# Half of a batch's experts run inside its own second attention instead of the next batch's first; gates are made per half; narrow mix blocks become wide

## The chip, the cores and the metric

One core of one Trainium2 chip runs the whole program. The time is microseconds on the device from the start to the end of one execution. Engines: PE is TensorE (matmuls, with their weight loads apart as PEld), DVE is VectorE, ACT is ScalarE, POOL is GpSimd, SP is SyncE, which here only issues DMAs. Each engine runs its own instructions in order and waits on semaphores.

## What is computed

A batch of 8 images of 256 channels and 32 x 32 positions (T = 1024 tokens) goes through three layers, each added to its input:

```python
x = x + proj(attention(qkv(group_norm(x))))        # 8 heads of 32, no mask, all 1024 keys
t = t + W_O(attention(layer_norm(t)))              # 8 heads of 32, causal
sel = sigmoid(layer_norm(t) @ expert_sel.T)        # 32 experts
w = top-2 of sel per token, else 0                 # gates, [token, expert]
h = relu(einsum('td,edh->teh', layer_norm(t), keys))   # hidden size 64
t = t + einsum('teh,te,ehv->tv', h, w, values)     # all experts computed, gated
```

## The kernel before, in words

The layout is channels on partitions: 256 channels are two tiles of 128 (CT), which are also the two groups of four heads (g = 0, 1). Tokens are cut in two halves of 512 (hf = 0, 1), and 8 tiles of 128. A weight product is split in high and low parts and needs three matmuls (`split`, L532 to L537).

The order of the work is written out by hand as a list of steps in the class `Steps` (L47 to L141); each engine walks the same list and does its share of each step, so the order of the list is the order on every engine and on SP's queue. There are four lists: `first`, `head` (batch 0, no experts), `body` (batches 1 to 7, a loop of seven trips, which starts with the experts of the batch before) and `last` (the experts of batch 7 alone). A count of steps gives each semaphore value.

The steps that matter here:
- `qk` (L617, L817, L1034): the query or key projection of one group and half: six matmuls on PE, the high part on ACT, the low part on DVE, both into `nat`. `stack` (L432): SP copies `nat` into `q_st` and `k_st` with 12 DMAs of 128 KB. A later q step writes over `nat` and so waits on ACT for the other group's copies (L820 to L826).
- `top` (L638, L1042): scores of one query tile for two heads in one of two two-bank PSUM buffers (`ps_two`), and DVE's row maximum over them. `peak` joins the two key halves, `row` (L658, L836) turns the maxima into a row of `q_st` with PE and ACT. In attention 1 (the causal one) half 0 has 8 tops a group and half 1 has 16, eight of them over fewer keys.
- `mix` (L673, L844): scores the other way round, exp on ACT, then values and sums on PE into `ps_acc`. A wide block takes two heads in a `ps_two` buffer and two exps of up to 1024 columns; a narrow block one head in a `ps_one` buffer and four exps of up to 512. The four mixes of attention 1 are e (g 0, hf 0, wide), f (g 1, hf 0, narrow), g (g 0, hf 1, narrow) and h (g 1, hf 1, wide). `norm`, `div` and `fin` divide by the sums, mostly on DVE.
- `out`, `lna`, `lnb`: output projection with the residual, then the layer norm of one half: mean, squares, mean of squares, inverse root.
- `logits`, `inputs`, `turn` (L726, L903, L456): selection scores of all 1024 tokens (16 matmuls, of which the trace shows 32 passes), top two on DVE; high part (ACT) and low part (POOL) of the layer norm's output; the gates turned by PE, written to DRAM with eight DMAs, waited for, and read back broadcast over partitions, two DMAs for each expert tile, four tiles ahead.
- `up` (L742, L917, L1137): one of 16 expert tiles (two experts each) for one half: six matmuls up, DVE's relu times gate (L1146), ACT's high part, DVE's low part (L965), and with a lag of two tiles six matmuls down into `ps_acc`. POOL makes low parts of keys and values (L510). `down` finishes the last two and adds to `x_res`; SP stores.

Memory is shared: `gated` and the broadcast gates lie in `probs`, where the exps go (L312, L318), and the experts' parts lie in `nat` (L314 to L317).

In `body` the 32 ups (both halves of batch it-1) are spread among 70 of the 80 top steps of attention 0 (L97 to L108). The narrow mixes f and g leave `ps_two` free, so that the tops of (1,0,1) stand among f's last block and a projection (L128), and those of (1,1,1) among g (L129 to L131). h has the output projection of half 0, its layer norm and the next batch's group norm among its blocks (L133, L134).

```python
ups = [("up", hf, j) for hf in range(self.halves) for j in range(self.experts)]
steps = spread(ups, tops) if tops else ups
...
e, f, g, h = (self.mix(1, g, hf, hf == g) for hf in (0, 1) for g in (0, 1))
```

## Time and profile before

| | |
|---|---|
| median of 3 runs | 3903.73 us (3895.03 to 3910.25) |
| the profiled execution | 3897.4 us |
| its span | 3895.7 us, mean granted PE clock 0.892 |
| busy share of the span | PE 87%, DVE 52%, ACT 43%, POOL 11% |
| one trip of the loop | about 475 us |

The page gives each engine's busy time as a share of the span and then in 40 equal slices; the clock line is what TensorE was granted in each slice, in tenths of 2.4 GHz, and a stretch is at 2.4 or at 1.2 GHz, so a tenth in between is a mixture. A row of a window says how long each engine was busy in that stretch. In a timeline, the bracket behind a row is the time for which the engine stood idle before it, and what it waited for. "Idle" alone does not cost anything on an engine that is not the bottleneck.

### The profile page before, as it was taken

Reading aid. Unit: us, or ns where it says so; the run is one execution under the profiler, and the core shown is the slowest. Engines: PE = TensorE matmul, PEld = TensorE weight load, DVE = VectorE, ACT = ScalarE, POOL = GpSimd, SP = SyncE. Lnnn points to the kernel's source line nnn. Section 1 sums busy time; section 2 is a strip of 40 time slices with the busy share of each in tenths; the row PEclk is TensorE's granted clock in tenths of the full one; section 3 lists DMA queues with packets and bytes.
Section 4 is the critical chain, followed back from the end, with each engine's and each line's share of the span. In section 5 each row is a group of like instructions: output and inputs, shape, how many; then the busy total and the mean of one; then the engine's idle time right before and its main releaser. Section 6 shows DMA issues by size and latency. Waiting matters only on the chain.

```text
span 3895.7 us, 54844 instructions
## 1 busy us (share of the span) xinstructions
PE 3380.4 (87%) x18386; PEld 1841.5 (47%) x18386; DVE 2022.0 (52%) x2825; ACT 1670.6 (43%) x2604; POOL 421.5 (11%) x539
## 2 busy tenths in 40 slices
PE   5898799987998879988799888998889988899779
PEld 2343464445634356343563445534465344554347
DVE  6434583356823568235672447624575254843544
ACT  1453335543364433644236343463434634345334
POOL 0000030001300013000230002200032000310005
PEclk7797899988999789988899898997889978999789
DMA  3011340114402043020530205202142022511125
GB/s 98 1 44 33 87 140 25 44 33 114 132 6 60 18 127 120 9 57 17 141 111 17 58 19 145 90 17 60 29 142 82 17 60 46 148 58 33 45 52 167
DMA packets 151948, 263.13 MB, mean 68 GB/s; under 512 B 26832, under 2 KB 28880, under 8 KB 151504
## 3 DMA queue, kind: packets, MB, share of 16 engines
q1 hardware_dynamic: 151632, 259.15, 24.6%
q8 instruction: 170, 2.79, 0.3%
q14 instruction: 146, 1.20, 0.1%
HBM read 145.80 MB, written 9.44 MB: 40 GB/s over the span
## 4 chain that ended last, share of the span: by engine, by line
PE 69%; DVE 13%; ACT 7%; issue 6%; SPq 3%; DMA 2%; DVEq 0%; POOL 0%; ACTq 0%; POOLq 0%
PE ps_acc L583 10%; PE ps_two L688 8%; PE ps_acc L592 8%; PE ps_one L535 7%; DVE tops L1050 7%; PE ps_two L652 6%; PE ps_one L537 5%; PE ps_one L536 5%; PE ps_one L688 3%; PE ps_acc L535 3%; PE ps_acc L536 3%; PE ps_acc L537 3%; SPq L448 2%; ACT stacks L840 2%; ACT probs L857 2%
## 5 line engine op out<-in xcount | busy, mean ns | idle before, releaser
L1050 DVE TENSOR_REDUCE tops<-ps_two 128x2 bf16<-128x1024 f32 (+3 forms) x896 | 964.4, 1112 | 431.8 <-PE ps_two L652 253.8
L857 ACT ACTIVATE probs<-ps_two 128x1024 f32<-128x1024 f32 (+1 forms) x704 | 642.3, 961 | 287.9 <-PE ps_two L688 220.4
L652 PE MATMUL ps_two<-stacks 32*128 32x512 f32 (+3 forms) x1792 | 426.9, 508 | 175.7 <-DVE tops L1050 135.4
L688 PE MATMUL ps_two<-stacks 97*128 97x512 f32 (+3 forms) x1408 | 462.7, 439 | 63.8 <-ACT probs L857 34.3
L583 PE MATMUL ps_acc<-probs,v_sb 128*32 128x512 f32 (+3 forms) x3584 | 474.8, 605 | 0.0
L510 POOL TENSOR_TENSOR nat<-expert_sb,nat 128x256 fp32r<-128x256 f32 x512 | 382.1, 747 | 644.1 <-ACT nat L801 546.7
L592 PE MATMUL ps_acc<-probs,ones 128*32 128x512 f32 (+3 forms) x3584 | 451.3, 578 | 0.0
L688 PEld LDWEIGHTS ps_two<-stacks 97*128 97x128 f32 x1408 | 250.1, 196 | 333.4 <-issue 187.9
L652 PEld LDWEIGHTS ps_two<-stacks 32*128 32x128 f32 x1792 | 172.4, 204 | 456.3 <-DVE tops L1050 230.6
L801 ACT CAST nat<-expert_sb 128x256 fp32r<-128x256 f32 x256 | 103.1, 406 | 616.3 <-DVE probs L1146 531.8
L516 POOL TENSOR_TENSOR act_lo<-xn,act_hi 128x2048 fp32r<-128x2048 f32 x8 | 36.1, 4509 | 2822.7 <-ACT act_hi L907 2822.7
L1064 DVE COPY rsum<-ps_acc 128x512 f32<-128x512 f32 x64 | 44.2, 691 | 543.3 <-PE ps_acc L592 543.3
L857 ACT ACTIVATE probs<-ps_one 128x512 f32<-128x512 f32 (+3 forms) x384 | 169.8, 488 | 196.0 <-PE ps_one L692 97.2
L535 PE MATMUL ps_one<-act_hi,nat 128*128 128x512 f32 x512 | 232.1, 453 | 23.4 <-POOL nat L510 23.4
L840 ACT CAST stacks<-ps_two 1x1024 fp32r<-1x1024 f32 x128 | 128.6, 1005 | 266.4 <-PE ps_two L669 263.5
L1146 DVE SCALAR_TENSOR_TENSOR probs<-ps_one,probs 128x512 f32<-128x512 f32 x256 | 175.8, 687 | 126.2 <-PE ps_one L537 77.8
L592 PEld LDWEIGHTS ps_acc<-probs,ones 128*32 128x32 f32 x3584 | 114.3, 117 | 222.7 <-issue 215.6
L535 PE MATMUL ps_one<-act_hi,w_hi 128*128 128x512 f32 x392 | 178.5, 455 | 45.8 <-DVE act_lo L1032 16.9
L535 PE MATMUL ps_acc<-nat 128*128 128x512 f32 x512 | 209.2, 409 | 1.1 <-POOL nat L510 0.9
L537 PE MATMUL ps_one<-act_hi,nat 128*128 128x512 f32 x512 | 208.9, 408 | 0.0
L536 PE MATMUL ps_one<-act_lo,nat 128*128 128x512 f32 x512 | 208.4, 407 | 0.0
L536 PE MATMUL ps_acc<-nat 128*128 128x512 f32 x512 | 205.6, 402 | 0.0
(127 smaller groups left out, 4476.2 us busy)
## 6 DMA issues: line engine op xcount, KB each, us to landing
stacks<-nat SPq DMA_DIRECT2D x792, 128.0 KB, 2.4
expert_sb<-experts_dram SPq DMA_DIRECT2D x256, 256.0 KB, 2.8
probs<-gates_dram SPq DMA_DIRECT2D x512, 128.0 KB, 3.0
x_in<-x_in_dram SPq DMA_DIRECT2D x9, 1024.0 KB, 5.0
out_dram<-x_res SPq DMA_DIRECT2D x16, 512.0 KB, 2.9
probs<-mats_dram SPq DMA_DIRECT2D x1, 2048.0 KB, 9.3
gates_dram<-w_turn SPq DMA_DIRECT2D x64, 16.0 KB, 1.6
sel_w<-sel_dram SPq DMA_DIRECT2D x1, 32.0 KB, 8.3
```

The lines of the kernel that those rows point to most:

```text
L510: pool.tensor_tensor(parts[:, 2 + m % 2, :], expert_sb[:, m % RING, c:c + C], f(parts[:, m % 2, :]), ALU.subtract).then_inc(lowered, 1)
L535: pe.matmul(acc, lh, rh, start=start, stop=False)
L536: pe.matmul(acc, lh, rl, start=False, stop=False)
L537: return pe.matmul(acc, ll, rh, start=False, stop=stop)
L583: pe.matmul(ps_acc[HD * j:HD * j + HD, 0, a:HALF], v_sb[:, k, c:c + HD], probs[:, sec.no["mix"][s] % 2, j, a:HALF], start=(k == 0), stop=( ...
L592: mm = pe.matmul(ps_acc[HD * j:HD * j + HD, 1, a:HALF], ones32[:], probs[:, sec.no["mix"][s] % 2, j, a:HALF], start=(k == 0), stop=(k == l ...
L652: mm = pe.matmul(acc[:, HALF * e:HALF * e + n_keys], q_st[rows, g, j, P * i:P * i + P], k_st[rows, g, j, HALF * kh:HALF * kh + n_keys], st ...
L688: mm = pe.matmul(at[:, a:HALF], k_st[0:MID + 1, g, j, P * k:P * k + P], q_st[0:MID + 1, g, j, HALF * hf + a:HALF * hf + HALF], start=True, ...
L840: done(act.copy(q_st[MID:MID + 1, g, 2 * pr:2 * pr + 2, half(hf)], acc[MID:MID + 1, :, :]), s)
L857: done(act.activation(probs[:, n % 2, per * i:per * i + per, a:HALF], acc[:, :, a:HALF], ACT.Exp, scale=SCALE), s + (i,))
L1050: done(dve.reduce_max(tops[:, kh, 2 * pr:2 * pr + 2, i], acc[:, :, 0:cols(st, i, kh)], AX_X), s)
L1146: done(dve.scalar_tensor_tensor(out=gated[:, r, :], in0=acc, scalar=0.0, in1=gate_bc[:, r, :], op0=ALU.max, op1=ALU.mult), s)
```

## The change

- `experts_of` takes one half. `body` and `last` run half 1 of the batch before; half 0 of the batch in hand runs in its own attention 1, so `head` has it too, and `last` has only half 1.
- Half 1's 16 ups are spread among the same 70 top steps of attention 0; half 0's 16 ups among 18 of the 20 steps of the tops of (1,1,1).
- All four mixes of attention 1 are wide. The projection (1,1,1) comes ahead of the tops of (1,0,1), and those stand among the norm, `out` and `lna` of half 0, without mix blocks. g has `lnb`, `logits`, `inputs` and `turn` of half 0 among its blocks, and no tops. h has `down` of half 0 and the next batch's group norm.
- Logits, inputs and turn are made for each half: 8 logit matmuls, half the tokens, four gate writes. For half 0 SP waits for g's last sum before it loads gates, and h's first two exps wait for `down` of half 0.
- Counts that were worked out (n of `qk`'s wait and others) now come from the list.

The diff, cut to its core:

```diff
--- before.py
+++ after.py
@@ -94,19 +94,16 @@
     def first(self):
         return [("stats",), ("gn",), ("split", 0), ("split", 1)] + self.qk(0, 0) + self.v(0)[:2]
 
-    def experts_of(self, tops):
-
-        ups = [("up", hf, j) for hf in range(self.halves) for j in range(self.experts)]
-        steps = spread(ups, tops) if tops else ups
-        at = steps.index(("up", 0, self.experts - 1)) + 1
-        behind = at + 2 if tops else at
-        return steps[:at] + [("lower", 0)] + steps[at:behind] + [("down", 0)] + steps[behind:] + [("lower", 1)]
+    def experts_of(self, hf, tops):
+
+        ups = [("up", hf, j) for j in range(self.experts)]
+        return (spread(ups, tops) if tops else ups) + [("lower", hf)]
 
     def batch(self, experts):
         tops = rows_later(self.top(0, 0, 0) + self.top(0, 0, 1) + self.top(0, 1, 0) + self.top(0, 1, 1))
         if experts:
-            steps = self.qk(0, 1, [0]) + [("logits",)] + self.v(0)[2:] + self.qk(0, 1, [1]) + [("inputs",)]
-            steps += tops[:3] + [("turn",)] + tops[3:10] + self.experts_of(tops[10:])
+            steps = self.qk(0, 1, [0]) + [("logits", 1)] + self.v(0)[2:] + self.qk(0, 1, [1]) + [("inputs", 1)]
+            steps += tops[:3] + [("turn", 1)] + tops[3:10] + self.experts_of(1, tops[10:])
         else:
             steps = self.v(0)[2:] + self.qk(0, 1) + tops
 
@@ -119,26 +116,28 @@
         t = rows_later(self.top(1, 0, 0))
         steps += d[3:5] + spread(d[5:8] + self.v(1)[:2], t)
 
-        e, f, g, h = (self.mix(1, g, hf, hf == g) for hf in (0, 1) for g in (0, 1))
+        e, f, g, h = (self.mix(1, g, hf, True) for hf in (0, 1) for g in (0, 1))
         t = rows_later(self.top(1, 1, 0))
         steps += e[:1] + [("norm", 0, 1, 1)] + self.qk(1, 1, [0]) + [("div", 0, 1, 1), e[1], e[2], ("fin", 0, 1, 1)]
         steps += [e[3]] + t[:3] + self.out(0, 1) + t[3:8] + [("lna", 0, 1)] + t[8:]
         steps += f[:1] + [("norm", 1, 0, 0), ("lnb", 0, 1), f[1], f[2], ("parts", 1), ("div", 1, 0, 0)]
-        steps += self.qk(1, 0, [1]) + [("fin", 1, 0, 0)] + self.v(1)[2:]
-        steps += spread([f[3]] + self.qk(1, 1, [1]), rows_later(self.top(1, 0, 1)))
-        m = [g[1], ("div", 1, 1, 0), g[2], ("fin", 1, 1, 0)] + g[3:]
+        steps += self.qk(1, 0, [1]) + [("fin", 1, 0, 0)] + self.v(1)[2:] + [f[3]] + self.qk(1, 1, [1])
+        t = rows_later(self.top(1, 0, 1))
+        steps += [("norm", 1, 1, 0)] + t[:2] + [("div", 1, 1, 0)] + t[2:5] + [("fin", 1, 1, 0)] + t[5:9]
+        steps += self.out(1, 0) + t[9:14] + [("lna", 1, 0)] + t[14:]
+        steps += g[:2] + [("lnb", 1, 0), g[2], g[3], ("logits", 0), g[4], ("inputs", 0), g[5], ("turn", 0), g[6], g[7]]
         t = rows_later(self.top(1, 1, 1))
-        steps += g[:1] + [("norm", 1, 1, 0)] + spread(m[:-1], t[:-1]) + [m[-1], t[-1]]
-
-        steps += h[:1] + [("norm", 1, 0, 1), h[1], ("div", 1, 0, 1), h[2], ("fin", 1, 0, 1), ("stats",), h[3]]
-        steps += self.out(1, 0) + [("gn",), h[4], ("lna", 1, 0), h[5], ("split", 0), ("lnb", 1, 0), h[6], h[7]]
+        m = self.experts_of(0, t[2:])
+        steps += t[:2] + [("norm", 1, 0, 1)] + m[:3] + [("div", 1, 0, 1)] + m[3:7] + [("fin", 1, 0, 1)] + m[7:]
+
+        steps += h[:1] + [("down", 0), h[1], ("stats",), h[2], ("gn",), h[3], h[4], ("split", 0), h[5], h[6], h[7]]
         steps += [("norm", 1, 1, 1), ("div", 1, 1, 1)] + self.qk(0, 0, [0]) + [("fin", 1, 1, 1)] + self.v(0)[:2]
         steps += self.out(1, 1)
         steps += [("split", 1), ("lna", 1, 1)] + self.qk(0, 0, [1]) + [("lnb", 1, 1)]
         return steps
 
     def last(self):
-        return [("logits",), ("inputs",), ("turn",)] + self.experts_of([]) + [("down", 1)]
+        return [("logits", 1), ("inputs", 1), ("turn", 1)] + self.experts_of(1, []) + [("down", 1)]
 
 
 
...
         if kind in ("norm", "down"):
             add("acc", s)
+        if kind == "down":
+            add(f"store{s[1]}", s)
         if kind in ("split", "parts", "inputs"):
             add("acts", s)
         if kind == "stack":
...
@@ -417,18 +425,21 @@
                 for s in sec.steps:
                     if s[0] == "logits":
 
-                        hold(acc_read, "acc", 0)
-                        for m in range(RING):
-                            load_expert(m)
+                        if s[1]:
+                            hold(acc_read, "acc", 0)
+                        elif sec.name == "body":
+                            hold(acc_read, "acc", sec.no["acc"][("down", 1)])
+                        for j in range(RING):
+                            load_expert(j)
                     if s[0] == "up":
-                        m = s[1] * ET + s[2]
-                        if 1 <= m and m - 1 + RING < NH * ET:
-
-                            read(("up",) + divmod(m - 1, ET))
-                            load_gates(m - 1 + RING)
-                        if m + RING < NH * ET:
-                            hold(vals_down, "up", m + 1)
-                            load_expert(m + RING)
+                        _, hf, j = s
+                        if 1 <= j and j - 1 + RING < ET:
+
+                            read(("up", hf, j - 1))
+                            load_gates(hf, j - 1 + RING)
+                        if j + RING < ET:
+                            hold(vals_down, "up", sec.no["up"][s])
+                            load_expert(j + RING)
                     if s[0] == "stack":
                         _, st, g, hf = s
 
...
@@ -454,25 +465,32 @@
...
                     if s[0] == "turn":
+                        hf = s[1]
                         read(s)
-                        for i in range(TT):
-                            sp.dma_start(w_dram[:, P * i:P * i + P],
-                                         w_turn[E * (i % PH):E * (i % PH) + E, i // PH, :]).then_inc(gates_out, 16)
-                        hold(gates_out, "turn", sec.no["turn"][s], 16 * TT)
-                        for m in range(RING):
-                            load_gates(m)
+                        for i in range(PH):
+                            at = HALF * hf + P * i
+                            sp.dma_start(w_dram[:, at:at + P], w_turn[E * i:E * i + E, hf, :]).then_inc(gates_out, 16)
+                        hold(gates_out, "turn", sec.no["turn"][s], 16 * PH)
+                        if hf == 0:
+
+                            hold(mixed, "mix", sec.no["mix"][last_mix(sec, ("norm", 1, 0, NH - 1))])
+                        for j in range(RING):
+                            load_gates(hf, j)
                     if s[0] == "down":
                         hf = s[1]
                         hold(acc_read, "acc", sec.no["acc"][s])
-                        where = out[B - 1:B] if sec.name == "last" else out[bass.ds(it - 1, 1)]
+                        if sec.name == "body":
+                            where = out[bass.ds(it - 1 if hf else it, 1)]
+                        else:
+                            where = out[B - 1:B] if hf else out[0:1]
                         sp.dma_start(where.rearrange("a (k p) t -> p (a k) t", p=P)[:, :, half(hf)],
                                      x_res[:, :, half(hf)]).then_inc(stored[hf], 16)
...
@@ -724,30 +744,26 @@
...
                     elif kind == "logits":
-                        pe.wait_ge(xn_ready, sec.value("lnb", 0))
+                        hf = s[1]
+                        pe.wait_ge(xn_ready, sec.value("lnb", normed(sec, hf)))
                         acc = bank(s)
-                        for i in range(TT):
+                        for i in range(PH):
+                            at = HALF * hf + P * i
                             for k in range(CT):
-                                mm = pe.matmul(acc[:, E * i:E * i + E], xn[:, k, P * i:P * i + P], sel_w[:, k, :],
+                                mm = pe.matmul(acc[:, E * i:E * i + E], xn[:, k, at:at + P], sel_w[:, k, :],
                                                start=(k == 0), stop=(k == CT - 1))
                         filled(mm, s)
...
@@ -851,6 +867,8 @@
                         if n <= 2 and sec.name == "body":
 
                             act.wait_ge(acc_read, sec.value("acc", sec.no["acc"][("down", NH - 1)]))
+                        if s[1:4] == (1, 1, NH - 1) and k < 2:
+                            act.wait_ge(acc_read, sec.value("acc", sec.no["acc"][("down", 0)]))
```

## Rows read from the trace of the kernel before

**Rows 1.** the page: busy time, granted clock in 40 slices, one DMA issue
```profile
PE 3380.4 (87%) x18386; PEld 1841.5 (47%) x18386; DVE 2022.0 (52%) x2825; ACT 1670.6 (43%) x2604; POOL 421.5 (11%) x539
...
PEclk7797899988999789988899898997889978999789
...
stacks<-nat SPq DMA_DIRECT2D x792, 128.0 KB, 2.4
```

**Rows 2.** windows of one trip: us, engines busy (instructions), PEclk, DMA share, GB/s
```profile
1428.00:1558.00 130.00, 123.04 (x548) 83.06 (x548) 107.22 (x129) 47.56 (x102) 46.40 (x63) 0.96 0.42 126
...
1712.00:1742.30 30.30, 25.23 (x144) 14.54 (x144) 11.14 (x16) 14.79 (x29) 0.00 (x0) 0.77 0.10 21
1742.30:1769.70 27.40, 18.75 (x76) 9.80 (x76) 17.59 (x20) 3.38 (x4) 0.00 (x0) 0.63 0.41 93
1769.70:1810.50 40.80, 36.09 (x240) 14.51 (x240) 19.27 (x23) 19.19 (x38) 0.00 (x0) 0.87 0.01 1
1810.50:1845.00 34.50, 33.17 (x220) 15.99 (x221) 17.83 (x40) 19.32 (x27) 0.00 (x0) 0.90 0.01 1
```

**Rows 3.** timeline, expert stage: start, us, engine, line, xcount, [idle before]
```profile
1444.18 0.50 PE L535 MATMUL ps_one<-act_hi,nat 128*128 128x512 f32 x1
...
1447.15 0.50 PE L652 MATMUL ps_two<-stacks 32*128 32x512 f32 x2
1447.58 0.50 PE L535 MATMUL ps_one<-act_hi,nat 128*128 128x512 f32 x1
...
1540.69 2.36 DVE L1050 TENSOR_REDUCE tops<-ps_two 128x2 bf16<-128x1024 f32 x2
1542.95 0.68 DVE L1146 SCALAR_TENSOR_TENSOR probs<-ps_one,probs 128x512 f32<-128x512 f32 x1
```

**Rows 4.** timeline, VectorE, tops alone in the batch ahead of the loop
```profile
76.10 2.36 DVE L1050 TENSOR_REDUCE tops<-ps_two 128x2 bf16<-128x1024 f32 x2
...
86.45 2.36 DVE L1050 TENSOR_REDUCE tops<-ps_two 128x2 bf16<-128x1024 f32 x2
```

**Rows 5.** windows, the same tops
```profile
56.00:138.20 82.20, 56.27 (x180) 23.07 (x180) 74.85 (x73) 7.03 (x7) 0.00 (x0) 0.50 0.14 32
```

**Rows 6.** timeline ahead of the expert stage: TensorE, SP, VectorE
```profile
1400.76 7.03 PE L731 MATMUL ps_one<-sel_w,xn 128*128 128x32 f32 x32 [5.41 <-DVE nat L1039]
...
1891.97 7.70 SPq L448 DMA_DIRECT2D stacks<-nat  x12
1899.86 4.11 SPq L459 DMA_DIRECT2D gates_dram<-w_turn  x8
...
1908.74 0.69 DVE L1146 SCALAR_TENSOR_TENSOR probs<-ps_one,probs 128x512 f32<-128x512 f32 x1 [5.65 <-DMA probs<-gates_dram]
```

**Rows 7.** groups by shape: xcount | busy us, mean ns | idle before
```profile
L857 ACT ACTIVATE probs<-ps_two 128x1024 f32<-128x1024 f32 x608 | 589.1, 1020 | 276.3 <-PE ps_two L688 220.4 <-DVE x_res L1156 43.8 <-PE ps_two L692 10.2
...
L510 POOL TENSOR_TENSOR nat<-expert_sb,nat 128x256 fp32r<-128x256 f32 x512 | 382.1, 747 | 644.1 <-ACT nat L801 546.7 <-ACT nat L927 84.0
...
L857 ACT ACTIVATE probs<-ps_one 128x512 f32<-128x512 f32 x192 | 105.7, 595 | 124.7 <-PE ps_one L688 95.1 <-PE ps_one L692 27.8
```

**Rows 8.** timeline around the tops of (1,0,1): stack copies, first top
```profile
1738.00 147.08 SPq L448 DMA_DIRECT2D stacks<-nat  x60
...
1744.37 1.56 DVE L1050 TENSOR_REDUCE tops<-ps_two 128x2 bf16<-128x1024 f32 x2 [5.86 <-PE ps_two L652]
```

**Rows 9.** timeline, TensorE in mix h: a mean, the last sums
```profile
1830.70 1.98 PE L718 MATMUL ps_one<-x_res,mean_w 128*128 128x512 f32 x4
...
1843.39 0.40 PE L592 MATMUL ps_acc<-probs,ones 128*32 128x128 f32 x8
```

**Rows 10.** timeline, TensorE after the first stage's last down
```profile
1566.07 0.73 PE L688 MATMUL ps_two<-stacks 97*128 97x512 f32 x2 [2.51 <-ACT probs L857]
```

**Rows 11.** windows, the closing section's second half of experts
```profile
3845.00:3892.40 47.40, 44.06 (x188) 34.19 (x186) 24.00 (x35) 19.13 (x46) 26.14 (x30) 1.00 0.48 152
```

**Rows 12.** windows, ten microseconds of the tail
```profile
1860.00:1870.00 10.00, 7.50 (x27) 4.83 (x27) 5.48 (x9) 3.58 (x5) 0.00 (x0) 1.00 0.31 69
```

More of the change, by code:

```diff
@@ L225, in value, with stacks_so_far @@
             return n * each
+        def stacks_so_far(self, s, g, hf):
+            return sum(t[0] == "stack" and t[2:] == (g, hf) for t in self.steps[:self.steps.index(s)])
         def any(self, kind, n):
@@ L255, in last_mix, with normed @@
         return next(m for m in sec.no["mix"] if m[1:5] == (st, g, hf, last_tile(st, hf)))
+    def normed(sec, hf):
+        return 0 if hf else sec.no["lnb"][("lnb", 1, hf)]
     def half(hf):
@@ L472, in _ @@
             last = Section("last")
-            sp.wait_ge(gates_out, last.value("turn", 1, 16 * TT))
-            for hf in range(NH):
-                sp.wait_ge(stored[hf], last.value("turn", 1, 16))
+            sp.wait_ge(gates_out, last.value("turn", 1, 16 * PH))
+            sp.wait_ge(stored[0], last.value("store0", 0, 16))
+            sp.wait_ge(stored[1], last.value("store1", 1, 16))
         @block.gpsimd
@@ L813, in emit @@
                         if sec.name != "first":
-                            read(("out", 1, hf, CT - 1))
+                            read(("out", 1, hf, CT - 1) if hf else ("up", hf, ET - 1))
                         act.copy(act_hi[:, :, half(hf)], xt[:, :, :]).then_inc(acts_hi, 1)
@@ L903, in emit @@
                     elif kind == "inputs":
-                        read(("qk", 0, 1, "k", 1) if sec.name == "body" else ("logits",))
-                        act.wait_ge(xn_ready, sec.value("lnb", 0))
-                        act.copy(act_hi[:, :, :], xn[:, :, :]).then_inc(acts_hi, 1)
+                        hf = s[1]
+                        if hf == 0:
+                            read(("out", 1, hf, CT - 1))
+                        else:
+                            read(("qk", 0, 1, "k", 1) if sec.name == "body" else ("logits", hf))
+                        act.wait_ge(xn_ready, sec.value("lnb", normed(sec, hf)))
+                        act.copy(act_hi[:, :, half(hf)], xn[:, :, half(hf)]).then_inc(acts_hi, 1)
                     elif kind == "turn":
@@ L1123, in emit @@
                         dve.sem_inc(passed, 1)
-                        for i in range(TT):
+                        for i in range(PH):
                             ins = dve.max(top8[:, i, :], pad_sel[:, i, 0:E])
@@ L1129, in emit @@
                         dve.sem_inc(passed, 1)
-                        for i in range(TT):
+                        for i in range(PH):
                             ins = dve.match_replace(rest[:, i, :], top8[:, i, :], pad_sel[:, i, :], 0.0)
```

129 lines of the change are left out of this document (61 added, 68 removed).

## The prediction

> **What bounds the kernel now.** I read the page first: TensorE is busy for 87% of the span, nothing else for more than 52%, and its granted clock is full in some slices and below 0.8 in others [rows 1]. So TensorE sets the pace where it is fed, and what a new order can win is the time in which it waits or runs at half clock. Then one trip of the batch loop, cut at its stages [rows 2]; the cuts span 475 us. Its stages: the expert stage (32 "up" steps among the first attention's row maxima, the "top" steps), the first attention's mixes (not shown; TensorE is all there is in them), mix f (group 1, half 0), the tops of (1,0,1), mix g (group 0, half 1) with the tops of (1,1,1), mix h (group 1, half 1), and a tail up to the next trip's first up (not shown). The reader should see three kinds. In the expert stage TensorE is busy 123 of 130 us at clock 0.96 and VectorE 107: nearly in balance. From f to g TensorE has holes and a clock of 0.63 to 0.87.
>
> **The price of a step.** At full clock an up (six matmuls up, six down) goes from 1444.18 to 1447.15, 2.97 us, and a top takes 0.43 [rows 3]. VectorE starts a top 1.13 us after the one before (two in 2.36, with their overlap) and needs some 1.28 for an up's two operations (0.68 each, overlapping) [rows 3]. Where tops stand alone, eight and their row take 76.10 to 86.45, 10.35 us, of which 8 x 1.13 is work and the rest, some 1.1, a bubble at the row [rows 4]; TensorE is granted 0.50 there over 82 us [rows 5].
>
> **Part 1: the expert stage loses 16 ups and keeps its tops.** TensorE loses 16 x 2.97 = 47 us of its 123, VectorE 16 x 1.28 = 20 and the 1.3 of the first "down", leaving 85.4 of 107.2 [rows 2, 3]. 47 us of TensorE work do not shorten a stage by 47 when VectorE then sets it. The first up also waits for its gates: 5.65 us of VectorE's idle time behind SP, which issues 12 stack copies, eight gate writes (4.1 us) and then the loads [rows 6]; with four writes this falls by 2 to 3.7. I add 3.5 for row bubbles that no up fills (seven rows at half of 1.1). 85.4 + 3.7 + 3.5 = 93 us instead of 130: **minus 37**. Bounds: 89 without bubbles, 106 if the clock falls (rivals).
>
> **Part 2: logits, inputs and turn are halved.** The logit matmuls (32 passes) take 7.0 us just ahead of the stage [rows 6]; half of them stay: minus 3.5, on the path. The halves of "inputs" on ScalarE and POOL are shorter too, but the gates come later than they do, so that counts nothing; were the gates not later, the next thing late would be the stack copies, which ScalarE awaits before it writes over their source.
>
> **Part 3: mix f wide.** Its 30 us hold TensorE 25 at clock 0.77 [rows 2], but most of the holes are the layer norm's chain between VectorE and ScalarE, which stays. An exp of 1024 columns is 1.02 us against twice 0.60 [rows 7]. I take minus 1; bounds 0 and minus 3.
>
> **Part 4: the tops of (1,0,1) lose their cover.** Now f's last block and a projection are spread among them, 27.4 us with VectorE busy 17.6 [rows 2]. After, the projection stands ahead of them. Its first ScalarE step must wait until the 12 copies of stack (1,0,1) have landed: issue begins at 1738.0 and twelve take 7.7, 2.4 more to land [rows 1], so about 1748 [rows 6, 8]. VectorE is in order, so the tops behind that wait begin at about 1750.5 and not at 1744.4 [rows 8]. Then it has 17.6 less the projection's two passes over 512 columns, 16.1, and nine such passes that are moved in between, at the 0.7 that one takes [rows 6] (the norm's copy, three of its division, "fin", two of "out", two of the mean's subtraction): 6.5, so 22.6. Two row bubbles and waits on a half-clock TensorE add 3, the last row and its copy 2. Mix g starts near 1778 where it starts at 1769.7. Less f's 1 us, already counted: **plus 7** (bounds plus 4, the same at full clock, and plus 12, if each wait falls in turn).
>
> **Part 5: mix g alone.** It takes 40.8 with 16 tops in it [rows 2]. The nearest mix is h, from 1810.5 to 1843.6, 33.1 us: it holds the 12 matmuls of "out" for half 0 (an up's number, 2.9) and the norm's two means (1.4 each until the next matmul starts; the row's 1.98 is with their overlap), so 27.3 for such a mix, some 2.6 of it lost to the half clock it starts at [rows 9]. For g without the values of the mix before, 26; plus the second mean 1.4, half the logits (3.5 at half clock, 1.8 at full: 2.6 taken). 30 us: **minus 11**.
>
> **Part 6: 16 ups among the tops of (1,1,1).** New: 16 x 2.97 = 47.5; 16 tops 6.8 (the short ones, with their masks, taken as the full ones' 0.43), two rows about 1.1. The last two downs (2.8) fall behind h's first block, so 52.6. SP waits for g's last sum before it loads gates, since they overwrite the exps; two loads 1.2 and 3 to land are 4.2, of which TensorE fills two ups' first halves: 2.5 stays. The last row's copy 1.4. **Plus 56.5**. VectorE has 16 x 1.28 and some 16 of tops, 37 us of work here, and does not set it. ScalarE, 48 us busy over 32 ups now [rows 2], and POOL, twice 0.75 per up [rows 7], are covered; bare, POOL's 24 us would come first.
>
> **Part 7: h.** It loses "out" and both means (5.8 of 33.1) and gains the two downs (2.8 at full clock) and the handover: its exps wait until the first down is added, as now after the first stage, where TensorE stands 2.5 us [rows 10]. It no longer starts at half clock (minus 2.6). -5.8 + 2.8 + 2.5 - 2.6: **minus 3**; bounds minus 6 and plus 1, with either wait gone or doubled.
>
> **Sum.** Per trip: -37 - 3.5 - 1 + 7 - 11 + 56.5 - 3 = +8 us; seven trips +56. The batch ahead of the loop gets parts 3 to 7: +48.5. The closing section runs one half of 16 ups for two: the second takes 47.4 us up to its store [rows 11]; less 3.5 of logits and 2.5 of gate writes and low parts ahead: -53. Total +51.5, on 3897.4 of the profiled execution 3949. The median shown lies 6.3 above that execution: **3955 us**, 1.3% slower. In words: the work is the same, the expert stage's own slack grows by 10 us a trip, the tops of (1,0,1) stand bare, and g and h return only part.
>
> **Rivals.**
> A. *The clock stays up where VectorE sets the pace* (the faster side). In the expert stage tops and ups alternate, and no stretch of tops is longer than four; for it: 1860 to 1870, in the tail, holds clock 1.00 at 7.5 us busy in ten [rows 12]. Then stage 89 (-4), part 4 -3, g's slow start -2.6, h's -1.4: 11 us less a trip, -3 instead of +8. 7 x -3, the head 41.5, the end -53: -32, so 3871. It decides from 8 us a trip on: below that the balance is not reached. Against: the clock is 0.63 in the tops of (1,0,1) already now, with a projection's matmuls among them, and 0.77 in f at 83% busy [rows 2].
> B. *The expert stage oscillates.* TensorE would be busy 71 of 93 us at full clock, in bursts between waits for two banks. If it is at half clock for half of the time, 71 needs 95, and each up (twice 2.97) outlasts the two tops and the up before that VectorE has in hand (3.5): 106 us instead of 93. 7 x 13 = 91: 4046. In half that degree 4000. The Trainium skill has this as a rule against the change (TensorE: Matmul & The Clock Gate, "A second HAM failure mode: psum-queue depth-cycling"): a TensorE that idles briefly between groups as PSUM banks come round keeps swapping its clock levels. By that rule the sum is 4000 or above, by the rows of the expert stage (0.96 at 95% busy) 3955; at 76% busy the trace has stretches of either kind [rows 2, 12].
> C. *Balance.* The bare tops cost no more than now (part 4 zero), since the copies' wait falls together with the 5.86 us for which VectorE idles there already [rows 8]: 8 x 7 = 56 less, 3899, no change. Against it, VectorE now works through five tops while the copies land, and after the change through none.
> That the change doesn't do what it says is excluded by the code: the steps are written out.
>
> **How the numbers follow.** Forecast 0.50 (own range 3925 to 3985), A 0.14, B 0.18, C 0.18. The forecast's lower tail falls to "no change" for 0.03, C gives 0.02 to each side. About 0.5%, 20 us, is what a measurement of this kernel can tell from no change. Faster 0.16, same 0.17, slower 0.67. The range leaves out most of A and the full B: 3888 to 4015.
>
> **What the changed profile would show.** Expert stage 93 us a trip with VectorE above 90% busy and a clock near 0.8 (A: 89 and 0.95; B: over 100 and below 0.75); 55 us from g's end to h's start with TensorE full; tops of (1,0,1) starting after 1750 of the old times and TensorE half idle; a closing section 47 us shorter. If the expert stage is shorter than 89, or g and its ups together shorter than 80 us, the forecast is wrong.

## The result and the profile after

The changed kernel takes **4167.3 us** (median of 4 runs, 4160.2 to 4168.7) beside 3904.9 (3895.0 to 3910.3): ratio 1.067, interval 1.0645 to 1.0687. The forecast was 3955 in a range of 3888 to 4015: the sign was right, the size wrong by 212 us, outside the range. The profiled execution spans 4165.1 us, 269.4 more than before, at a mean clock of 0.868 instead of 0.892.

The page of the changed kernel: busy times, granted clock by slice, and the costliest group with its idle time:

```profile
PE 3451.8 (83%) x18386; PEld 1908.9 (46%) x18386; DVE 2030.7 (49%) x2865; ACT 1657.4 (40%) x2428; POOL 419.2 (10%) x547
...
PEclk7798979988899887989889897898987979789798
...
L1070 DVE TENSOR_REDUCE tops<-ps_two 128x2 bf16<-128x1024 f32 (+3 forms) x896 | 961.9, 1112 | 367.3 <-PE ps_two L675 182.7
```

As many TensorE instructions as before (18386) are now busy for 71 us more: the work has not grown, and more of it runs at the half clock. To find where, I marked each trip by what SP issues: the gate writes of half 1 (G1), the store of half 1 (S1), the load of the next x (X), the gate writes and the store of half 0 (G0, S0). Means of the seven trips (changes taken before rounding):

| stretch | before | after | change | forecast |
|---|---|---|---|---|
| G1 to S1: expert stage, part 1 | 138.9 | 129.9 | -9.0 | -37 |
| S1 to X: first attention's mixes and on, mix e, not touched | 140.5 | 140.4 | -0.1 | 0 |
| X to the next G1: parts 2 to 7 | 193.9 | 241.4 | +47.6 | +45 |
| trip | 473.3 | 511.8 | +38.5 | +8 |

Seven trips make 269 of the 269.4 us. What stands ahead of the first G1 grew by 50.0 us (forecast 45: 48.5 less the 3.5 of the logits), what stands behind the last one shrank by 49.8 (forecast 49.5: 53 less the same 3.5). So of the 30.5 us a trip that the forecast missed, 28 lie in **one stage**.

The stages of one trip of the changed kernel (windows, as in [rows 2]): expert stage, mix f, tops of (1,0,1), mix g, half 0's ups with the tops of (1,1,1):

```profile
1553.93:1674.97 121.04, 93.25 (x355) 59.45 (x355) 86.15 (x94) 27.21 (x53) 22.61 (x32) 0.78 0.20 61
1834.40:1863.07 28.67, 25.41 (x165) 16.07 (x166) 10.72 (x15) 12.48 (x19) 0.00 (x0) 0.84 0.16 37
1863.07:1897.25 34.18, 17.56 (x85) 9.44 (x81) 23.28 (x29) 6.78 (x9) 0.00 (x0) 0.72 0.37 93
1897.25:1926.61 29.36, 28.68 (x181) 12.71 (x182) 7.66 (x24) 15.91 (x22) 3.77 (x3) 0.86 0.01 3
1926.61:1984.50 57.89, 53.03 (x264) 37.18 (x261) 39.95 (x55) 24.32 (x52) 22.47 (x30) 1.00 0.41 128
```

Four of the five are near the forecast (28.7, 34.2, 29.4 and 57.9 us). The first is not: 121 where 93 stood. VectorE has the work that the forecast gave it (86.2 us for 85.4); for the other 35 us it stands idle. Its groups there, before and after (line, out<-in, shapes, count | busy, mean ns | idle before them, releasers), first before (1428 to 1558):

```profile
L1050 DVE TENSOR_REDUCE tops<-ps_two 128x2 bf16<-128x1024 f32 x56 | 66.9, 1227 | 9.6 <-PE ps_two L652 8.4 <-issue 0.4
L965 DVE TENSOR_TENSOR nat<-probs,nat 128x512 fp32r<-128x512 f32 x32 | 22.1, 692 | 0.7 <-ACT nat L926 0.7
L1146 DVE SCALAR_TENSOR_TENSOR probs<-ps_one,probs 128x512 f32<-128x512 f32 x32 | 21.9, 686 | 11.7 <-PE ps_one L537 6.2 <-DMA probs<-gates_dram 5.4
```

and after (1553.9 to 1675):

```profile
L1070 DVE TENSOR_REDUCE tops<-ps_two 128x2 bf16<-128x1024 f32 x55 | 64.8, 1226 | 18.6 <-PE ps_two L672 18.5
L1166 DVE SCALAR_TENSOR_TENSOR probs<-ps_one,probs 128x512 f32<-128x512 f32 x16 | 11.1, 691 | 16.6 <-PE ps_one L557 11.3 <-DMA probs<-gates_dram 5.1
L985 DVE TENSOR_TENSOR nat<-probs,nat 128x512 fp32r<-128x512 f32 x16 | 10.9, 682 | 0.0
```

With half of the ups, VectorE waits twice as long for TensorE: 18.5 + 11.3 us instead of 8.4 + 6.2. The gates' wait stayed at 5 us (5.4 before; the forecast let it fall to about 3.7). What TensorE does meanwhile, from its timeline (start, us, line): an up that is at half clock from its start to its end, between two tops.

```profile
1616.46 0.80 PE L555 MATMUL ps_one<-act_hi,nat 128*128 128x512 f32 x1
1617.05 0.63 PE L556 MATMUL ps_one<-act_lo,nat 128*128 128x512 f32 x1
...
1621.32 0.63 PE L557 MATMUL ps_acc<-nat 128*128 128x512 f32 x1
1621.88 0.77 PE L672 MATMUL ps_two<-stacks 32*128 32x512 f32 x4
```

This up takes 5.42 us where it took 2.97 [rows 3]. It is one of the slowest. Of the 98 ups in the seven stages whose twelve matmuls stand together (14 a trip), 17 take 4.8 us and more, 42 some 4.5 (part of the up at half clock), 39 some 3.0; the mean is 4.00 us, against 3.03 before. VectorE's timeline beside the slow one:

```profile
1614.45 3.49 DVE L1070 TENSOR_REDUCE tops<-ps_two 128x2 bf16<-128x1024 f32 x3 [0.60 <-PE ps_two L672]
1619.61 0.69 DVE L1166 SCALAR_TENSOR_TENSOR probs<-ps_one,probs 128x512 f32<-128x512 f32 x1 [1.67 <-PE ps_one L557]
1620.21 0.68 DVE L985 TENSOR_TENSOR nat<-probs,nat 128x512 fp32r<-128x512 f32 x1
1622.46 1.23 DVE L1070 TENSOR_REDUCE tops<-ps_two 128x2 bf16<-128x1024 f32 x1 [1.56 <-PE ps_two L672]
```

VectorE has three tops in hand, works them off, and waits 1.67 us for the up and 1.56 for the top behind it. That is rival B's picture, at more than the price that it named.

### The profile page after: what moved, and what is told of

The parts are those of the page before. It is cut to its first block, busy times and chain, and to the rows that moved or that the text cites. A ratio compares the mean times of both kernels' runs of the same rounds, so it can differ in the third digit from the quotient of the medians.

```text
span 4165.1 us, 54390 instructions
## 1 busy us (share of the span) xinstructions
PE 3451.8 (83%) x18386; PEld 1908.9 (46%) x18386; DVE 2030.7 (49%) x2865; ACT 1657.4 (40%) x2428; POOL 419.2 (10%) x547
## 4 chain that ended last, share of the span: by engine, by line
PE 64%; DVE 15%; issue 7%; ACT 6%; SPq 5%; DMA 2%; DVEq 0%; POOL 0%; ACTq 0%; POOLq 0%
PE ps_two L708 11%; PE ps_acc L603 9%; DVE tops L1070 9%; PE ps_acc L612 8%; PE ps_one L555 6%; PE ps_one L557 5%; PE ps_one L556 5%; PE ps_two L672 5%; SPq L459 4%; PE ps_acc L555 3%; PE ps_acc L556 3%; PE ps_acc L557 3%; ACT probs L875 2%; PE ps_one L744 2%; ACT stacks L856 1%
## 5 line engine op out<-in xcount | busy, mean ns | idle before, releaser
L875 ACT ACTIVATE probs<-ps_two 128x1024 f32<-128x1024 f32 (+3 forms) x896 | 788.0, 929 | 427.1 <-PE ps_two L708 234.2
L672 PE MATMUL ps_two<-stacks 32*128 32x512 f32 (+3 forms) x1792 | 449.2, 529 | 313.0 <-DVE tops L1070 283.2
L708 PE MATMUL ps_two<-stacks 97*128 97x512 f32 (+3 forms) x1792 | 609.6, 449 | 96.7 <-ACT probs L875 49.5
L708 PEld LDWEIGHTS ps_two<-stacks 97*128 97x128 f32 x1792 | 335.9, 205 | 432.2 <-issue 228.0
L603 PE MATMUL ps_acc<-probs,v_sb 128*32 128x512 f32 (+3 forms) x3584 | 462.6, 590 | 0.0
L817 ACT CAST nat<-expert_sb 128x256 fp32r<-128x256 f32 x256 | 102.3, 406 | 757.5 <-DVE probs L1166 675.0
L536 POOL TENSOR_TENSOR act_lo<-xn,act_hi 128x1024 fp32r<-128x1024 f32 x16 | 37.9, 2367 | 2698.0 <-ACT act_hi L929 2698.0
L555 PE MATMUL ps_one<-act_hi,nat 128*128 128x512 f32 x512 | 254.7, 497 | 40.4 <-POOL nat L528 40.3
L555 PE MATMUL ps_acc<-nat 128*128 128x512 f32 x512 | 226.7, 443 | 13.5 <-DVE nat L985 12.9
L557 PE MATMUL ps_one<-act_hi,nat 128*128 128x512 f32 x512 | 232.5, 454 | 0.0
L556 PE MATMUL ps_one<-act_lo,nat 128*128 128x512 f32 x512 | 231.1, 451 | 0.0
L946 ACT CAST nat<-probs 128x512 fp32r<-128x512 f32 x256 | 158.3, 618 | 179.7 <-PE ps_acc L557 176.3
L556 PE MATMUL ps_acc<-nat 128*128 128x512 f32 x512 | 221.3, 432 | 0.0
```

The lines of the kernel that those rows point to most:

```text
L555: pe.matmul(acc, lh, rh, start=start, stop=False)
L556: pe.matmul(acc, lh, rl, start=False, stop=False)
L557: return pe.matmul(acc, ll, rh, start=False, stop=stop)
L603: pe.matmul(ps_acc[HD * j:HD * j + HD, 0, a:HALF], v_sb[:, k, c:c + HD], probs[:, sec.no["mix"][s] % 2, j, a:HALF], start=(k == 0), stop=( ...
L672: mm = pe.matmul(acc[:, HALF * e:HALF * e + n_keys], q_st[rows, g, j, P * i:P * i + P], k_st[rows, g, j, HALF * kh:HALF * kh + n_keys], st ...
L708: mm = pe.matmul(at[:, a:HALF], k_st[0:MID + 1, g, j, P * k:P * k + P], q_st[0:MID + 1, g, j, HALF * hf + a:HALF * hf + HALF], start=True, ...
```

## The experiments

Two theories. **CLOCK**: spread 3.4 to an up (4.4 steps), the tops leave TensorE idle so often that its clock falls; at half clock it is late for VectorE each time, and that is where the 28 us a trip go. **ORDER**: up and top wait for each other through banks and in-order queues, whatever the clock is, and fewer ups for the same tops only lose overlap. All runs are beside the kernel before on the same chip (its median 3902 to 3906). "Stage" is the mean of seven trips, from 3 us after the gates' write to 8 us before half 1's store; it is 127.9 us before (clock 0.96 to 0.98) and 118.9 after. "An up" is the mean time of an up in it, as counted above: its twelve matmuls, until the next other one starts.

| run | edit of the changed kernel | us | ratio (95%) | stage | its clock | an up |
|---|---|---|---|---|---|---|
| the change | | 4167.3 | 1.0645-1.0687 | 118.9 | 0.77-0.83 | 4.00 |
| e1_fill1 | 1 added matmul per top | 4103.8 | 1.0478-1.0537 | 113.1 | 0.85-0.92 | 3.29 |
| e5_fill2 | 2 added matmuls per top | 4145.0 | 1.0606-1.0648 | 112.0 | 0.93-0.98 | 2.88 |
| e6_apart | ups first, then the 70 steps | 4162.2 | 1.0644-1.0683 | 118.6 | 0.67-0.70 | 2.89 |
| e9_dense | ups among first 18 steps | 4097.8 | 1.0462-1.0523 | 109.7 | 0.73-0.75 | 2.95 |
| e2_bunch | ups among first 35 of 70 | 4043.9 | 1.0315-1.0374 | 102.3 | 0.76-0.80 | 2.99 |
| e11_fifty | ups among first 50 | 4110.4 | 1.0476-1.0546 | 111.9 | 0.75-0.81 | 3.59 |
| e10_late | ups among last 35 | 4007.5 | 1.0230-1.0291 | 96.3 | 0.77-0.80 | 3.02 |
| e3_cover | projection among tops (1,0,1) | 4141.8 | 1.0565-1.0655 | 118.0 | 0.77-0.84 | 3.94 |
| e8_both | e2 and e3 | 4056.8 | 1.0366-1.0417 | 104.2 | 0.76-0.80 | 3.07 |
| e12_late_cover | e10 and e3 | 3989.2 | 1.0178-1.0235 | 96.6 | 0.77-0.80 | 3.04 |
| e4_narrow | mixes f, g narrow again | 4187.3 | 1.0671-1.0754 | 117.7 | 0.77-0.84 | 3.92 |
| e7_wide | kernel before, f and g wide | 3978.2 | 1.0165-1.0211 | 129.1 | 0.95-0.97 | 3.08 |

**More work for TensorE (e1_fill1, e5_fill2).** The added matmuls belong to no result; they are extra work. The trace has 52 (104 in e5) of them a trip: tops ahead of the first up and behind the last get none. At the 0.23 us of the expectation they are 12 and 24 us.

```diff
+ at = sec.steps.index(s)          # in "top", before its matmuls
+ ups = [t for t in sec.steps[at:] if t[0] == "up"]
+ if st == 0 and sec.name == "body" and len(ups) < 2 * ET and ups and ups[0][1] == 1:
+     idle = bank(ups[0])
+     for _ in range(1):           # e5: range(2)
+         pe.matmul(idle, w_hi[:, 0, 0, 0:P], w_hi[:, 0, :, :].rearrange("p k c -> p (k c)"), start=True, stop=True)
```

> The changed kernel, with one more matmul (128 x 128 weights, 512 columns, result unused) ahead of every top of the expert stage; it goes into the ps_one bank that the next up overwrites, so nothing new waits. Theory CLOCK (the stage takes 121 us and not 93 because the granted clock falls to 0.77 between the ups, and an up at half clock, 5 to 6 us, outlasts the two tops and one up that VectorE has in hand): the clock rises above 0.93 and the stage falls to 97 to 105 us in spite of 56 x 0.23 = 13 us of added work; whole kernel 4167 - 7 x 20, about 4030. Theory ORDER (every up in TensorE's in-order stream holds the tops back by some 1.8 us whatever the clock): the stage stays at 118 to 124 us or grows by the added work; 4150 to 4250.

> The changed kernel with two extra matmuls (128x128x512, into a bank that the next up clears) ahead of each top of the expert stage, where the run before had one (that gave 4104 us, a clock of 0.85 to 0.92 in the stage, and a stage 6 us shorter in spite of 13 us of added work). The work added is 26 us per trip at full clock. CLOCK: the stage costs what it does because TensorE works at the half clock in it; with two the granted clock of the stage is 0.95 or more, TensorE is then the bound with some 106 us of work, and the stage is 107 to 109 us instead of 121: 4085 us (4070 to 4105). ORDER (steps wait for each other whatever the clock): added work only adds; 26 us a trip on the present 121, less what falls into waits, 4190 to 4300 us.

Both kernels do more and are faster than the changed one, by 64 and by 22 us. ORDER has no room for that: it gave 4150 to 4250 and 4190 to 4300. But both miss CLOCK's number as well (about 4030, and 4070 to 4105). With one filler half-clock stretches remained, 26 of 98 ups are still slow; with two none is, and TensorE is the bound. Two windows of e5_fill2's stage:

```profile
1566.00:1576.00 10.00, 10.00 (x42) 6.17 (x41) 7.52 (x9) 2.06 (x4) 1.46 (x2) 1.00 0.29 100
1576.00:1586.00 10.00, 10.00 (x46) 5.75 (x44) 7.40 (x10) 3.67 (x7) 2.91 (x4) 1.00 0.18 56
```

Its stage has 107 us of TensorE work, one more than expected, and takes 112, not 107 to 109. So no run here shows the even spread at full clock without added work, and how much of its loss would be left there is open. Another 3 us a trip went after the stage (S1 to X is 143.6 instead of 140.4); in one trip a window there reads clock 0.93 where the changed kernel has 1.00. Why it fell there was not tried.

**Spreading against bunching (e2_bunch, e9_dense, e11_fifty, e6_apart).** Only the length of the list that the ups are spread over differs:

```diff
-            steps += tops[:3] + [("turn", 1)] + tops[3:10] + self.experts_of(1, tops[10:])
+            steps += tops[:3] + [("turn", 1)] + tops[3:10] + self.experts_of(1, tops[10:45]) + tops[45:]
```

(e9: 28 for 45; e11: 60 for 45; e6: `self.experts_of(1, []) + tops[10:]`)

> The changed kernel, with half 1's 16 ups spread among the first 35 of the 70 top steps of the expert stage (the density that the 32 ups had before) and the other 35 steps alone behind them. CLOCK: the dense part keeps the clock at 0.95 and takes 16 x 4.06 = 65 us as before the change, the bare part 28 tops at 10.35 us for eight = 36, at half clock, which costs nothing there: 101 us, whole kernel 4167 - 7 x 20, about 4030. ORDER: 16 times the same hold, wherever the ups stand: 114 to 121 us, 4120 to 4170.

> The changed kernel with half 1's 16 ups among the first 18 of the 70 steps of the expert stage, 52 alone behind them (1.1 steps per up; with 35, 2.2 per up, it was 4044 us, with all 70, 4.4 per up, 4167 us). CLOCK: the ups' part holds the full clock, as with 35, and takes the 47.5 to 52 us that unmixed ups take, the tops left alone run at VectorE's pace whatever the clock, 42 at 1.29 us are 54: a stage of 104 us instead of 102, 4060 us (4045 to 4080). ORDER (the less mixed, the more is lost): half way between 4044 and the 4162 of the ups taken out altogether, about 4100.

> The same with 50 of the 70 steps among the ups (3.1 per up) and 20 alone. By work alone: VectorE has some 75 us in the mixed part and TensorE 67, so at full clock VectorE bounds it and 17 tops alone follow, 22 us, 97 us in all, 4015 us (4000 to 4030). CLOCK says that this holds only if TensorE is busy enough to keep the clock; if it falls in the mixed part as it does with 70, the stage is 105 to 120 us, 4065 to 4160. ORDER has no reason for a step between 35 and 50: between 4015 and 4044.

> The changed kernel with the 16 ups of half 1 ahead of the 60 remaining steps of the first attention's maxima instead of spread among them. Nothing lies beside anything: 47.5 us of ups (the closing section, where they stand alone at full clock) and 56 tops at 10.35/8 us, 72 us, make 120 us, which is what the changed kernel's mixed stage takes (121). CLOCK: a bare run of ups holds the full clock and a bare run of tops does not need it, so 4160 us (4140 to 4185): spreading hides nothing. ORDER: the spread steps do hide some of each other (each up's VectorE part beside its matmuls), taking them apart costs 10 us a trip or more, 4235 us and above.

(70 steps stand behind the ups in e6, 55 of them tops, not the 60 and 56 of the expectation.) e6_apart puts nothing beside anything and takes the changed kernel's time: as it stood, the spreading of the change gained nothing over doing one after the other. CLOCK gave 4140 to 4185, ORDER 4235 and above. Windows of 10 us, e6_apart (us, then PE, PEld, DVE, ACT, POOL busy, PEclk): ups alone, then the handover, then tops alone.

```profile
1566.00:1576.00 10.00, 10.00 (x46) 8.26 (x45) 4.58 (x8) 4.87 (x12) 6.18 (x7) 1.00 0.63 190
...
1606.00:1616.00 10.00, 6.02 (x22) 2.55 (x22) 9.11 (x9) 0.72 (x1) 0.00 (x0) 0.62 0.00 0
1616.00:1626.00 10.00, 6.91 (x26) 3.01 (x24) 9.41 (x9) 0.65 (x2) 0.00 (x0) 0.50 0.01 2
1626.00:1636.00 10.00, 7.01 (x24) 2.78 (x22) 9.35 (x9) 0.63 (x1) 0.00 (x0) 0.50 0.00 0
```

Bare tops hold VectorE at 9.35 to 9.41 of ten at half clock, so they can lose 0.6 us in ten by it at most. Ups lose more. In the changed kernel the two share every stretch, and the clock goes up and down:

```profile
1563.00:1573.00 10.00, 8.29 (x22) 5.01 (x21) 7.08 (x9) 1.64 (x4) 1.45 (x2) 0.50 0.20 69
1573.00:1583.00 10.00, 8.21 (x33) 5.01 (x32) 5.28 (x8) 3.05 (x6) 2.18 (x3) 0.77 0.17 52
1583.00:1593.00 10.00, 7.27 (x28) 4.83 (x29) 9.39 (x10) 1.54 (x4) 2.17 (x3) 0.91 0.32 94
1593.00:1603.00 10.00, 7.85 (x30) 5.22 (x29) 6.08 (x7) 2.33 (x4) 1.46 (x2) 0.67 0.22 67
...
1623.00:1633.00 10.00, 7.55 (x38) 5.24 (x39) 8.70 (x11) 2.24 (x4) 2.16 (x3) 1.00 0.34 107
```

VectorE has 9.39 and 8.70 of ten at clock 0.91 and 1.00, and 5.28 to 7.08 where it is 0.50 to 0.77. In e2_bunch (4044 us, about 4030 expected by CLOCK, 4120 and more by ORDER) there are 2.2 steps to an up, as before the change, and then bare tops:

```profile
1540.00:1550.00 10.00, 9.21 (x46) 6.49 (x45) 8.19 (x11) 3.57 (x7) 3.45 (x5) 1.00 0.45 145
1550.00:1560.00 10.00, 10.00 (x45) 6.80 (x44) 9.24 (x12) 3.80 (x9) 4.42 (x6) 1.00 0.41 131
...
1600.00:1610.00 10.00, 7.02 (x26) 3.04 (x24) 9.01 (x10) 1.00 (x1) 0.00 (x0) 0.50 0.00 0
```

The mean clock is no higher than in the changed kernel (0.76 to 0.80), but 96 of the 98 ups are fast, and the trip is 16.7 us shorter from G1 to S1: what counts is which work gets the full clock. e9_dense and e11_fifty lie on either side and both lose. In e9 the dense part is TensorE's alone (16 ups and the 14 tops among them are 47.5 + 6 us; I had left those 6 out, and the 4060 missed) while VectorE has 7.5 of ten. In e11, where work alone said 97 us, the clock falls in the mixed part, as CLOCK allowed (two of its windows):

```profile
1556.00:1566.00 10.00, 8.27 (x31) 5.90 (x32) 6.41 (x7) 2.36 (x5) 2.17 (x3) 0.74 0.32 92
1566.00:1576.00 10.00, 8.90 (x31) 5.84 (x30) 6.22 (x9) 2.35 (x6) 2.19 (x3) 0.75 0.25 73
```

ORDER gave 4015 to 4044 for it; 4110 was measured. Among 35, 50 and 70 steps the stage takes 102.3, 111.9 and 118.9 us and an up 2.99, 3.59 and 4.00.

**Bare tops first (e10_late).**

```diff
-            steps += tops[:3] + [("turn", 1)] + tops[3:10] + self.experts_of(1, tops[10:])
+            steps += tops[:3] + [("turn", 1)] + tops[3:45] + self.experts_of(1, tops[45:])
```

> The changed kernel with the same bunching as the run of 4044 us, turned round: 35 of the steps alone first, then the 16 ups among the last 35. CLOCK: the same two parts in the other order, the clock at half in the first and full in the second, 4044 us (4030 to 4065). If the gain of the bunched run came instead from the ups being early (their expert loads and the half's store leave sooner, the stack transfers get SP sooner), it is gone: 4120 to 4170.

4007 us, 36 better than the same bunch at the front (CLOCK had expected no difference) and 160 better than the change. The rival, a gain from early ups, had 4120 to 4170 and is out. The first two rows are how e2_bunch's stage opens, the others e10_late's at its handover from tops to ups and behind it:

```profile
1520.00:1530.00 10.00, 7.03 (x26) 3.99 (x25) 5.78 (x7) 1.51 (x4) 1.72 (x3) 0.56 0.53 143
1530.00:1540.00 10.00, 9.67 (x44) 6.29 (x43) 9.46 (x12) 5.14 (x12) 5.07 (x8) 1.00 0.56 172
```

```profile
1546.00:1556.00 10.00, 8.68 (x32) 4.78 (x30) 7.45 (x8) 2.14 (x4) 0.65 (x1) 0.60 0.00 0
1556.00:1566.00 10.00, 9.78 (x47) 6.53 (x47) 9.58 (x12) 4.27 (x11) 4.93 (x8) 1.00 0.56 151
```

Tops ahead of the ups cover the wait for the gates. In e2_bunch VectorE's step for the ups waits 4.1 us on the gates; in e10_late's stage its groups show no such wait, and 7.5 + 4.3 us on TensorE. Over the seven trips VectorE waits 4.3 us a trip less for gates, ups and tops together, most of the 6.0 us between the two stages. First e2_bunch, then e10_late:

```profile
L1166 DVE SCALAR_TENSOR_TENSOR probs<-ps_one,probs 128x512 f32<-128x512 f32 x16 | 11.0, 687 | 6.7 <-DMA probs<-gates_dram 4.1 <-PE ps_one L557 2.6
```

```profile
L1070 DVE TENSOR_REDUCE tops<-ps_two 128x2 bf16<-128x1024 f32 x54 | 63.4, 1225 | 7.8 <-PE ps_two L672 7.5
L1166 DVE SCALAR_TENSOR_TENSOR probs<-ps_one,probs 128x512 f32<-128x512 f32 x16 | 11.0, 685 | 4.7 <-PE ps_one L557 4.3 <-issue 0.3
```

The stage is 96.3 us with VectorE busy 84, and G1 to S1 is 31.7 us shorter than before the change where the forecast had 37: another order of the same steps comes within 5.3 us a trip of it.

**The smaller parts (e3_cover, e8_both, e12_late_cover, e4_narrow, e7_wide).** e3 takes part 4's loss of cover back:

```diff
-        steps += self.qk(1, 0, [1]) + [("fin", 1, 0, 0)] + self.v(1)[2:] + [f[3]] + self.qk(1, 1, [1])
+        steps += self.qk(1, 0, [1]) + [("fin", 1, 0, 0)] + self.v(1)[2:] + [f[3]]
         t = rows_later(self.top(1, 0, 1))
-        steps += [("norm", 1, 1, 0)] + t[:2] + [("div", 1, 1, 0)] + t[2:5] + [("fin", 1, 1, 0)] + t[5:9]
+        q = self.qk(1, 1, [1])
+        steps += [("norm", 1, 1, 0)] + t[:2] + [("div", 1, 1, 0)] + t[2:5] + q[:1] + [("fin", 1, 1, 0)] + t[5:7] + q[1:] + t[7:9]
```

> The changed kernel, with the projection (1,1,1) and its stack moved from ahead of the tops of (1,0,1) to among them: q after the fifth top step, k and stack after the seventh. If the 10.2 us for which VectorE stands in front of the first tops are the wait of the projection's ScalarE step for the copies of stack (1,0,1), VectorE starts on the tops 4 to 6 us sooner: 4167 - 8 x 5, about 4127. If the tops' stage is paced by TensorE at half clock anyway (its projection and out now fall among the tops), nothing: 4160 to 4175.

> The changed kernel with two of the earlier edits together: half 1's ups among the first 35 of the 70 steps (alone 4044 us) and the projection (1,1,1) among the tops of (1,0,1) (alone 25 us off). They lie in different stretches, so CLOCK expects the sum, 4019 us (4005 to 4035). Rival: what one gives the other takes (SP or the stack transfers that both wait for), 4044 us.

> The changed kernel with 35 steps alone, then the 16 ups among the last 35 (alone 4007 us), and the projection (1,1,1) among the tops of (1,0,1) (by itself 25 us off, but 13 us on when added to the bunch that begins at once, where three of the seven trips had a stage of 106.6 instead of 101.2 us, as the clock came up later after the first ups). If that loss belongs to where the first ups meet a clock that is still at half, it stays away here, since the stage begins with tops that need no clock: 3990 us (3982 to 4000). Rival: the cover itself costs what it gives once the ups are bunched, 4007 to 4020 us.

e3 gives 25 us, in runs that lie far apart (4128 to 4161, the change 4160 to 4169); 2.4 us a trip come from X to G0, half of what was expected there. Added to e2 it does not help: e8 is 13 us slower than e2 by the medians, though the runs overlap (4046 to 4062, e2 4035 to 4050), and CLOCK's 4005 to 4035 missed. Three of e8's seven stages take 106.5 to 106.9 us and the shortest 101.1; in e2 one of seven took 106.7. Windows of 5 us at the start of a long and of a short stage of e8_both:

```profile
1022.00:1027.00 5.00, 4.29 (x16) 2.83 (x16) 1.16 (x2) 0.52 (x3) 1.26 (x2) 0.50 0.46 139
1027.00:1032.00 5.00, 5.00 (x15) 3.01 (x14) 2.48 (x4) 2.88 (x6) 2.06 (x3) 0.50 0.61 170
1032.00:1037.00 5.00, 5.00 (x18) 3.48 (x17) 3.57 (x5) 1.48 (x4) 1.59 (x3) 0.70 0.38 112
```

```profile
1522.50:1527.50 5.00, 4.70 (x18) 3.08 (x19) 1.57 (x2) 0.84 (x3) 1.21 (x3) 0.59 0.53 150
1527.50:1532.50 5.00, 5.00 (x23) 3.28 (x24) 4.11 (x6) 2.63 (x6) 2.61 (x4) 1.00 0.57 167
```

The full clock comes later after the same first ups in the long one; why was not found. With bare tops ahead of the ups the loss stayed away: e12_late_cover met its expectation, 3989 us, the best form of the change that was found and still 2.1% slower than the kernel before.

e4_narrow undoes the wide form:

```diff
-        e, f, g, h = (self.mix(1, g, hf, True) for hf in (0, 1) for g in (0, 1))
+        e, f, g, h = (self.mix(1, g, hf, hf == g) for hf in (0, 1) for g in (0, 1))
```

> The changed kernel, with mixes f and g narrow again (four exps of 512 columns from the two ps_one banks in place of two of 1024 from ps_two), nothing else. By the forecast's term for f (1 us) and 32 narrow exps of 0.595 for 16 wide of 1.02 in g (2.7 us of ScalarE, only partly on the path), 1 to 4 us a batch: 4175 to 4200. Rival: narrow blocks also share the ps_one banks with the norm, the logits and turn, which now stand in g, and TensorE waits for each: 5 us or more a batch, above 4207. If widening gained nothing, 4160 to 4172.

> The kernel before with nothing moved, only its two narrow mixes of the second attention (f and g) made wide. If the wide form is worth something by itself: f 1 us a trip, g 2 to 4 us, 3875 us (3860 to 3890). Rival: g's wide blocks take their banks from the pool of the tops that are spread among them, each waits for the other, 3 us a trip more, 3925 us.

e4 is 20 us slower than the change, as expected (its runs 4169 to 4197): with the tops of (1,1,1) out of g, wide f and g together are worth some 3 to 4 us a trip (from X to the next G1, 245.2 us narrow and 241.4 wide). e7 gives the kernel before the same wide blocks and loses 75 us, more than either of its numbers (3875, and 3925 for the rival); its trips are 11 us longer. Mix g with the tops of (1,1,1) in it takes 52.7 us in e7, from 1798.83 to the first matmul of h at 1851.57, against 40.8 us [rows 2], and VectorE waits 25.5 us there for tops, 15.5 before. The window, and VectorE's group in e7 and in the kernel before:

```profile
1798.83:1851.57 52.74, 41.83 (x241) 18.12 (x241) 19.27 (x23) 17.71 (x22) 0.00 (x0) 0.74 0.00 1
```

```profile
L1050 DVE TENSOR_REDUCE tops<-ps_two 128x2 bf16<-128x1024 f32 (+3 forms) x16 | 15.8, 1026 | 25.5 <-PE ps_two L652 25.5
```

```profile
L1050 DVE TENSOR_REDUCE tops<-ps_two 128x2 bf16<-128x1024 f32 (+3 forms) x16 | 15.8, 1026 | 15.5 <-PE ps_two L652 15.5
```

The 11.9 us in g are as much as the whole trip lost. Wide blocks and tops take the same `ps_two` banks, and the clock is 0.74 instead of 0.87. Which of the two costs more was not taken apart. The wide form of g pays only with its tops gone; the tops can go without it, as in e4, for 20 us.

## Why the prediction was wrong

- **Part 1 failed: minus 37 forecast, minus 9 measured.** The step that failed is "85.4 + 3.7 + 3.5 = 93 us", which took VectorE as the bound and let it idle for 7 us. The work was right (86.2), and so was the mean clock (near 0.8 forecast, 0.77 to 0.83 measured). What failed is the overlap: a lower clock was to cost nothing behind VectorE, which was to be over 90% busy. It was 71% busy (86.15 of 121.04 us), since ups of 4.00 us in the mean, some of 5.42, came later than it had tops in hand; it waited 18.5 us for tops, 11.3 for ups and 5.1 for gates. e10_late has the same work with ups of 3.02 us, and VectorE waits 21.8 us less a trip for ups, gates and tops; its G1 to S1 is 22.7 us shorter than the change's, 159 of the 160 us between those two kernels. The clock is shown as a cause by the added matmuls; how the 22.7 us split between faster ups and the order by itself is not.
- **Rival B named the mechanism and bounded it too low.** It gave 106 us for half clock in half of the time, which is a mean of 0.75; the clock read 0.77 to 0.83, so less of the time than that, and still the stage took 119 to 121. B priced only the up that outlasts what VectorE has in hand; the top behind it comes late as well (1.56 us beside 1.67 in the timeline). The Trainium skill (TensorE: Matmul & The Clock Gate, "A second HAM failure mode: psum-queue depth-cycling") describes a kernel whose TensorE idles briefly between groups as PSUM banks come round, so that its clock goes back and forth between the two levels. The prediction took that as a rule against the change, and this case's traces agree: windows of 10 us read 0.50 to 1.00, and added matmuls made the kernel faster. I gave it 0.18. Of the rows at such a busy share I counted one of either kind [rows 2, 12]; the one with tops in it, the tops of (1,0,1) at 0.63 [rows 2], was the nearer, and it spoke for B.
- **What I leaned on instead was the neighbour.** The expert stage before, 0.96 at 95% busy, was a poor row for one that would be 76% busy: the change took out half of the ups among the same tops. With the old ratio of tops to ups (e2_bunch) the clock was back at 1.00 in that part.
- **Parts 2 to 7 stand**, each by itself (one trip). Forecast +45, measured +47.6. Part 2: the logit matmuls take 3.6 us instead of 7.0, -3.4 for -3.5. Part 3: f, from its first matmul to the first top, 28.7 us instead of 29.2, -0.5 for -1, though it now holds a projection more. Part 4: from the first top of (1,0,1) to g 34.2 us instead of 25.9, +8.3 for 7 to 8 (VectorE idles 10.21 us behind the projection's ScalarE step, which waits for the stack copies). Part 5: g 29.4 for 30. Part 6: 57.9 for 56.5, at clock 1.00. Part 7: h 30.2 instead of 33.2, -3.0 for -3.

```profile
1867.04 1.41 DVE L1059 SCALAR_TENSOR_TENSOR nat<-ps_one,bias,nat 128x512 fp32r<-128x512 f32 x2 [10.21 <-ACT nat L844]
```

- **Ahead of the first G1** +50.0 us for 45; where these 5 us lie was not traced. **Rivals A and C** fell: the clock did not stay up, and the bare tops cost their 8 us.
- With part 1 as measured, the forecast's own sum is 3955 + 7 x 28 = 4151, 16 under the median.
